# A decoder layer on one core: attention outputs turned by VectorE instead of TensorE, and maximum products placed between two score pairs

## Chip, cores and metric

The kernel runs on one NeuronCore of one Trainium2 chip. The metric is the device time of one launch in microseconds (us), the median of several runs. A batch of 8 sequences is worked on, all in float32 except where bfloat16 is named.

## The reference, cut to what matters

```python
x = _layernorm(x + _L0_attn_ref(x, ...))        # self-attention with decays by level
x = _layernorm(x + _L0_xattn_ref(x, ctx_1024, ctx_1024, Wq, Wk, Wv, Wo, bo))
x = _layernorm(x + _L0_ffn_ref(x, gate_w, gate_b, w1, w2))   # 32 experts, 8 tokens each

def _L0_xattn_ref(q, k, v, Wq, Wk, Wv, Wo, bo):  # 8 x 512 queries, 8 x 1024 keys, D = 256
    qh, kh, vh = ...                             # 16 heads of 16
    attn = softmax(einsum('bnhc,bmhc->bhnm', qh, kh) * 16 ** -0.5)
    return einsum('bhnm,bmhc->bnhc', attn, vh).reshape(B, QL, 256) @ Wo.T + bo
```

The gate of the last part takes a softmax over the 512 tokens of a batch for each of 32 experts and picks its 8 largest; each expert runs on its merged tokens, and the result is scattered back.

## The kernel before, in words

Three blocks follow each other: `self_attention`, `cross_attention`, `experts_and_combine`. In a block each engine has its own program, written out by hand, and they meet at semaphores; between blocks all engines meet. No planner sorts anything: the order of an engine's work is the order of the code.

The change sits almost wholly in `cross_attention`. Its `body` is called for the sections `pro`, `first` (batch 0), `mid` (batches 1 to 6), `last` (batch 7) and `tail` (what is left of batch 7). A batch is 32 steps `s`: four quads of heads (`q = s // 8`), eight chunks of 128 keys in each. In each step

- TensorE makes two score pairs (L1459: two heads each, transposed scores of 128 keys by 512 queries, into one of two slots `cpsA`), which ScalarE turns into probabilities (L1586, exp, 1.02 us a pair);
- TensorE makes four maximum products (L1398: queries by keys for step `s + 12`, `LEAD`), one at a time into one of three slots `cpsV`; VectorE takes the row maximum of each (L1680) and so empties the slot. Two of them stand behind the score pairs, two at the step's end;
- TensorE adds the values of the step before (L1420, four heads beside each other) into the one accumulator `acc`, 32 rows per head, 512 queries long. Every eighth step begins a new quad and needs `acc` empty.

The maxima of a quad go through a small chain (L1685 to L1701, then the transfer of `nmT` by SyncE, L1286) into three extra rows of the query stack, which the scores of that quad need 12 steps later; TensorE waits for that at steps 0, 8, 16 and 24.

When a quad is done, ScalarE copies `acc` to `OT` (L1616); one step later (`OUTPUTS = 1`) TensorE transposes it back to queries by features (L1439, four 128x128 blocks), VectorE divides by the row of sums (L1708, L1712) into `O`. At step 2 of the next batch (`MERGE`) TensorE transposes the whole `O` (L1360), ScalarE copies it to `oT` (L1558), and at step 4 (`PROJECT_O`) eight matmuls (L1475, four jobs, each needing a `cpsV` slot) give the output projection. VectorE adds the residual, the layer norm follows, then `X2T` (step 9: transposes of the normed tokens, L1522), `GATE` (step 12: two matmuls into 32 rows of 512, L1482; then the eight maxima, L1757), `TOP8` (step 20) and the picking of tokens (28, 29). The next batch is prepared beside it: `x1T` at step 0, the values of the second half of the heads at 1 (L1385), the queries at 4 (L1376), the keys at 7 and 12 (L1368), the values of the first half at 20. Each of these sends a 1024-wide result through a `cpsA` slot and a ScalarE copy of 1.01 us.

SyncE issues every transfer in one order, and waits in it: `stack_later` is twelve transfers that spread queries and keys of the next batch over the stack (L200, L201), `stack_max` is the transfer of `nmT`. In `last` and `tail` SyncE also loads the first experts' weights, 4 MB at a time (L1165).

## Time and profile before

| | |
|---|---|
| median of 3 runs (range) | 1839.48 us (1838.58 to 1839.82) |
| profiled execution: its time, its span | 1839.74 us, 1837.9 us |
| TensorE, VectorE, ScalarE, GpSimd busy | 91%, 67%, 46%, 33% of the span |
| mean granted TensorE clock | 0.953 of full speed |
| moved by transfers | 141.44 MB, mean 77 GB/s |

Self-attention lasts to about 589 us, the change of blocks to 629, the cross-attention's prologue to 660, batches 0 to 7 to 1643, the tail of batch 7 to 1677, the experts to 1804, the last layer norm to the end. A timeline row gives start, duration, engine, line, what is written and read, and in brackets how long the engine sat idle before it and whose end released it. `x4` merges four instructions; a busy TensorE overlaps its neighbours in these rows, so distances between starts are what to read.

### The profile page before, as it was taken

How to read it: one execution, taken by the hardware profiler on the slowest of the kernel's cores; microseconds unless marked ns; L12 is line 12 of the kernel's file. 1: busy time of each engine (PE TensorE's matmuls, PEld its weight loads, DVE VectorE, ACT ScalarE, POOL GpSimd, SP SyncE). 2: the span in 40 equal slices, each digit the busy share in tenths (PEclk: the TensorE clock that was granted, in tenths of full speed). 3: DMA queues.
4: the chain of work that ended last, by engine and by line, in shares of the span. 5: the costliest groups of instructions: out<-in, count | busy, mean ns of one | idle time of the engine just before them, and what ended most of it. 6: DMA issues, size and time to landing. Idle time of an engine off the chain costs nothing. (4 is left out here: it accounts for less than half of the span.)

```text
span 1837.9 us, 48963 instructions
## 1 busy us (share of the span) xinstructions
PE 1678.5 (91%) x19924; PEld 806.8 (44%) x19924; DVE 1232.9 (67%) x2424; ACT 838.3 (46%) x1015; POOL 598.2 (33%) x970
## 2 busy tenths in 40 slices
PE   5999999999999699999999999999999999976564
PEld 3566666666665333343333433433433334223332
DVE  5767677677674777868778788788687787812005
ACT  2334344344333136655646565566556465651103
POOL 3545545645625536043043061250430420000002
PEclk8999999999999779999999999999999999987777
DMA  7000000000000221111202101112112024046995
GB/s 252 3 4 4 3 3 3 3 3 3 3 32 15 69 67 50 41 38 59 83 1 85 56 28 65 50 38 69 35 64 78 1 89 183 30 179 267 421 418 183
DMA packets 62205, 141.44 MB, mean 77 GB/s; under 512 B 11280, under 2 KB 34320, under 8 KB 54320
## 3 DMA queue, kind: packets, MB, share of 16 engines
q1 hardware_dynamic: 61520, 137.88, 20.6%
q8 instruction: 157, 2.57, 0.6%
q10 hardware_dynamic: 480, 0.59, 0.1%
q14 instruction: 48, 0.39, 0.1%
HBM read 92.43 MB, written 7.86 MB: 55 GB/s over the span
## 5 line engine op out<-in xcount | busy, mean ns | idle before, releaser
L1680 DVE TENSOR_REDUCE mx<-cpsV 128x1 f32<-128x512 f32 x1024 | 655.2, 686 | 187.5 <-PE cpsV L1398 175.3
L1586 ACT ACTIVATE w<-cpsA 128x1024 f32<-128x1024 f32 x512 | 496.3, 1021 | 246.0 <-PE cpsA L1459 240.8
L1398 PE MATMUL cpsV<-w 96*128 96x512 bf16 x1024 | 325.4, 394 | 21.6 <-DVEq L1663 13.0
L1459 PE MATMUL cpsA<-w 99*128 99x512 bf16 x1024 | 275.2, 382 | 22.4 <-DMA w<-nmT 10.1
L1420 PE MATMUL cacc<-w 128*32 128x512 f32 x2048 | 279.7, 607 | 0.4 <-ACT w L1586 0.4
L468 PE MATMUL psA<-w 128*128 128x512 f32 x512 | 257.0, 625 | 5.0 <-DVE WT L1102 1.8
L1398 PEld LDWEIGHTS cpsV<-w 96*128 96x128 bf16 x1024 | 86.1, 98 | 283.4 <-DVE mx L1680 197.0
L1648 POOL TENSOR_TENSOR crstd<-cmv,eps 128x4 f32<-128x4 f32 x8 | 1.6, 202 | 605.8 <-DVE cmv L1746 605.8
L765 ACT COPY w<-psA 128x1024 f32<-128x1024 f32 x64 | 64.8, 1012 | 229.3 <-PE psA L468 229.3
L1459 PEld LDWEIGHTS cpsA<-w 99*128 99x128 bf16 x1024 | 93.0, 98 | 163.0 <-ACT w L1564 15.8
L885 POOL TENSOR_TENSOR VP<-V,VPF 128x128 f32<-128x128 f32 (+2 forms) x256 | 129.2, 535 | 42.7 <-PE psA L481 36.8
L1111 DVE TENSOR_TENSOR tmp<-psV,CF 128x512 f32<-128x512 f32 x64 | 44.3, 692 | 121.7 <-PE psV L531 121.4
L468 PEld LDWEIGHTS psA<-w 128*128 128x128 f32 x512 | 87.9, 191 | 76.5 <-issue 67.7
L183 POOL TENSOR_TENSOR w<-w,zero 128x256 bf16<-128x256 f32 x88 | 51.1, 612 | 138.8 <-ACTq L1565 138.8
L1420 PEld LDWEIGHTS cacc<-w 128*32 128x32 f32 x2048 | 42.5, 108 | 92.5 <-issue 74.5
L2031 DVE TENSOR_TENSOR z<-psE,b1T 128x256 f32<-128x256 f32 x8 | 3.4, 424 | 110.5 <-PE psE L1967 110.5
L1981 PE MATMUL psE<-w,hT 128*32 128x256 f32 x512 | 39.6, 477 | 36.5 <-DMA w<-in_w 34.6
L1564 ACT COPY w<-cpsA 128x1024 f32<-128x1024 f32 x21 | 21.3, 1012 | 111.5 <-PE cpsA L1368 59.9
L1118 DVE TENSOR_REDUCE w<-tmp 128x128 f32<-128x512 f32 x64 | 67.8, 1059 | 4.7
L501 PEld LDWEIGHTS psV<-w 64*32 64x32 f32 x4096 | 41.2, 106 | 49.8 <-issue 48.1
L1385 PEld LDWEIGHTS cpsA<-w,w 128*128 128x128 f32 x480 | 54.7, 192 | 12.6 <-ACT w L1586 12.6
L192 POOL TENSOR_TENSOR w<-w 128x256 bf16<-128x256 f32 x88 | 57.1, 680 | 3.1
(224 smaller groups left out, 2227.6 us busy)
## 6 DMA issues: line engine op xcount, KB each, us to landing
w<-in_w SPq DMA_DIRECT2D x56, 1024.0 KB, 16.3
w<-w SPq DMA_DIRECT2D x189, 128.0 KB, 2.3
w<-w SPq DMA_DIRECT2D x189, 64.0 KB, 2.0
w<-in_ctxT SPq DMA_DIRECT2D x8, 1024.0 KB, 5.0
w<-in_xT SPq DMA_DIRECT2D x8, 512.0 KB, 6.4
x_tok<-in_x SPq DMA_DIRECT2D x8, 512.0 KB, 9.7
w<-in_w SPq DMA_DIRECT2D x8, 512.0 KB, 17.2
out_y<-w SPq DMA_DIRECT2D x16, 256.0 KB, 2.3
```

What stands on the lines that cost most here:

```text
L183: ops.tensor_tensor(cut(high, m), cut(r, m), zeros, ALU.add)
L192: ops.tensor_tensor(cut(low, m), cut(r, m), cut(mid, m), ALU.subtract)
L468: last = nc.tensor.matmul(out[:, n * T:(n + 1) * T], w[:, k, i * P:(i + 1) * P], XT[:, b, k, :], start=(k == 0), stop=(k == KD - 1))
L765: nc.scalar.copy(QK[:, i % 4, :], full(("qk", i))).then_inc(act_evac, 1)
L885: last = nc.gpsimd.tensor_tensor(VP[:, p % 2, g, 0:n, :].rearrange("q n (h c) -> q n h c", c=HD), vv.unsqueeze(1).broadcast_to([P, n, 2, HD]),
L1118: nc.vector.tensor_reduce(yp, tmp[:].rearrange("p g s c -> p g c s"), AX_X, ALU.add)
L1385: last = nc.tensor.matmul(out[:, c * P:(c + 1) * P], cT[:, k, c * P:(c + 1) * P], wv[:, k, hv * P:(hv + 1) * P], start=(k == 0), stop=(k = ...
L1398: nc.tensor.matmul(out, Qst[q // 2][0:ROWS, hh, g * P:(g + 1) * P], Kst[q // 2][0:ROWS, hh, half * BANK:(half + 1) * BANK], start=True, st ...
L1420: last = nc.tensor.matmul(acc[BLK * jj:BLK * (jj + 1), :], Vc[:, chunk, 4 * q + jj, :], Pr[:, (2 * s + jj // 2) % 4, (jj % 2) * T:(jj % 2 ...
L1459: last = nc.tensor.matmul(out[:, n * T:(n + 1) * T], Kst[q // 2][0:ROWS + 3, hh, chunk * P:(chunk + 1) * P], Qst[q // 2][0:ROWS + 3, hh, : ...
L1586: nc.scalar.activation(Pr[:, (2 * s + pp) % 4, :], src, ACT.Exp, scale=CA_SCALE).then_inc(act_evac, 1)
L1680: nc.vector.tensor_reduce(mx[:, q % 2, row, k % 2:k % 2 + 1], full(m[k]), AX_X, ALU.max).then_inc(dve_evac, 1)
```

## The change

The outputs of a quad are no longer transposed by TensorE. The values of a head are laid at every second column of its 32 (with the ones at column 1). After the quad's last step VectorE reads `acc` itself and transposes it in 32x32 blocks to `byq` (`take_outputs`); this also frees `acc`. Later (`outputs`) it divides and transposes back to `byd`, and SyncE moves 64 of the 128 rows to their place in `oT` (`move_o`). The divisions of quads 0 to 3 stand at steps 12 and 20 of the batch, and both at step 1 of the next (in `last`, quad 2 at step 27). The output projection is two jobs instead of four. The gate's product is four groups of 32 rows by 128, at step 11, brought to 32 rows of 512 by four transfers before the maxima at step 12. The transposes of `X2T` are two jobs. In steps 1, 2, 5, 8, 10, 13 and 21 the first two maximum products stand between the two score pairs. The store of `x2` to memory moves ahead of the third `nmT` transfer. In the tail TensorE runs 130 transposes whose results nobody reads. In the tail of self-attention GpSimd adds `lnb` ahead of its norm factors, and VectorE multiplies by `lng` instead of GpSimd.

```diff
-OUTPUTS, X1T, PROJECT_V1, PROJECT_Q, MERGE, PROJECT_O, NORM = 1, 0, 1, 4, 2, 4, 7
-PROJECT_K, X2T, COPY_X2, GATE, GATE_EXP, TOP8, TOP8_T, PICK, PICK_T = (7, 12), 9, 10, 12, 14, 20, 21, 28, 29
-PROJECT_V0 = 20
+X1T, PROJECT_V1, PROJECT_Q, PROJECT_O, NORM = 0, 1, 4, 4, 7
+PROJECT_K, X2T, COPY_X2, GATE, GATE_MAX, GATE_EXP, TOP8, TOP8_T, PICK, PICK_T = (7, 12), 9, 10, 11, 12, 14, 20, 21, 28, 29
+PROJECT_V0, LAST_OUTPUTS = 20, 27
+BEHIND_JOBS = (X1T + 1, PROJECT_V1 + 1, PROJECT_Q + 1, PROJECT_K[0] + 1, X2T + 1, PROJECT_K[1] + 1, PROJECT_V0 + 1)
...
+                    if sec == "tail" and r == 0:
+                        pool.wait_ge(dve_evac, SA_DVE.count(sec, b, ("out", 1)) + DVE_SLOTS)
+                        add_lnb()
...
-                        dve.wait_ge(n1_scaled, b)
+                        if sec == "tail":
+                            dve.wait_ge(n1_ready, b * 2 - 1)
+                            nc.vector.tensor_tensor(n1[:], n1[:], lng[:].unsqueeze(1).broadcast_to([P, G, D]), ALU.mult)
+                            dve.drain()
+                        else:
+                            dve.wait_ge(n1_scaled, b)
...
-        if s % KT == OUTPUTS and (now and s > KT or prev and s < KT):
-            v.append(("otr", (s // KT - 1) % QUADS))
         if prev:
-            v += [("wo", g) for g in range(G) if s == PROJECT_O]
+            v += [("wo", r) for r in range(2) if s == PROJECT_O]
...
+        byq = [sb(f"byq_{n}", [P, KT * 2, BLK]) for n in range(2)]
+        byd = [sb(f"byd_{n}", [P, T]) for n in range(2)]
+        rec = sb("rec", [P, KT * 2])
...
+            def move_o(bb, q):
+
+                sp.wait_ge(o_ready, bb * QUADS + q + 1)
+                sp.dma_start(oT[64 * (q % 2):64 * (q % 2) + 64, q // 2, :], byd[q % 2][0:P:2]
+                             ).then_inc(o_moved[q % 2], 16)
...
+                if prev:
+                    if sec != "tail":
+                        move_o(b - 1, 2)
+                    move_o(b - 1, 3)
+                if now:
...
+                    sp.wait_ge(l4_ready, b)
+                    for g in range(G):
+                        sp.dma_start(L[:, g * P:(g + 1) * P], L4[E * g:E * (g + 1)]).then_inc(l_moved, 16)
...
                     stack_max(b, 2)
+                    move_o(b, 0)
...
                     sp.dma_start(sh.p8_dram[:, bass.ds((b - 1) * T, T)], P8).then_inc(p8_saved, 16)
                 if now:
+                    move_o(b, 1)
                     if nxt:
                         stack_later(b + 1, 1, free=CA_ACT.count(sec, b, ("s", 16, 1)))
...
                         stack_max(b + 1, 0)
                     else:
+                        move_o(b, 2)
                         sp.wait_ge(act_full, CA_ACT.count(sec, b, ("s", STEPS - 1, 1)))
                         load_group_weights(sp, sh, dram, 1, 1, EG)
                         sp.wait_ge(av_done, B * STEPS)
...
+                def keep_clock(count):
+
+                    if sec == "tail":
+                        for _ in range(count):
+                            nc.tensor.transpose(acc[:, 0:P], sh.ident[:], sh.ident[:])
...
+                            if maxima and pp == (0 if s in BEHIND_JOBS else 1):
+                                max_scores(s + LEAD, 0, 1)
+
+                    if sec == "tail" and s == 1:
+                        pe.wait_ge(acc_evac, b * QUADS + 1)
+                        keep_clock(34)
...
-                            evacuated_a("oT")
-                            for g in range(G):
-                                out = take_v(("wo", g))
-                                for k in range(KD):
-                                    last = nc.tensor.matmul(out[:, 0:D], oT[:, k, g * P:(g + 1) * P], wo[:, k, :],
-                                                            start=(k == 0), stop=(k == KD - 1))
+                            for of in o_moved:
+                                pe.wait_ge(of, b * 32 + 16)
+                            for r in range(2):
+                                out = take_v(("wo", r))
+                                for g in range(2):
+                                    for k in range(KD):
+                                        last = nc.tensor.matmul(out[:, g * D:(g + 1) * D],
+                                                                oT[:, k, (2 * r + g) * P:(2 * r + g + 1) * P], wo[:, k, :],
+                                                                start=(k == 0), stop=(k == KD - 1))
                                 last.then_inc(dve_full, 1)
+                            keep_clock(28)
...
+                            evacuated_a(("x2T", 1))
                             for k in range(KD):
-                                last = nc.tensor.matmul(out[0:E, :], gw[:, k, :], x2T[:, k, :],
-                                                        start=(k == 0), stop=(k == KD - 1))
+                                for g in range(G):
+                                    last = nc.tensor.matmul(out[E * g:E * (g + 1), 0:P], gw[:, k, :],
+                                                            x2T[:, k, g * P:(g + 1) * P], start=(k == 0), stop=(k == KD - 1))
                             last.then_inc(dve_full, 1)
+                            keep_clock(52)
...
-                    if prev and s == MERGE:
-                        pe.wait_ge(o_ready, b * QUADS)
-                        transpose_x("oT", O)
...
-                        nc.scalar.copy(OT[:], acc[:]).then_inc(acc_evac, 1)
...
+                def take_outputs(bb, q):
+
+                    dve.wait_ge(av_done, (bb * QUADS + q + 1) * KT)
+                    nc.vector.transpose(byq[q % 2][:].rearrange("p c s -> p (c s)"), acc[:]).then_inc(acc_evac, 1)
                     dve.drain()
-                    ov = O[:].rearrange("p g (h c) -> p g h c", c=HD)
-                    for g in range(G):
-                        last = nc.vector.tensor_tensor(ov[:, g, 4 * q:4 * q + 4], src[:, g, :, 0:HD],
-                                                       rec[:, g].unsqueeze(2).broadcast_to([P, 4, HD]), ALU.mult)
-                    dve.drain().then_inc(o_ready, 1)
-                    dve.nop().then_inc(dve_evac, 1)
+
+                def outputs(bb, q):
+
+                    t = byq[q % 2]
+                    nc.vector.reciprocal(rec[:], t[:, :, 1])
+                    dve.drain()
+                    nc.vector.tensor_tensor(t[:, :, 0:BLK:2], t[:, :, 0:BLK:2], rec[:].unsqueeze(2).broadcast_to([P, KT * 2, HD]),
+                                            ALU.mult)
+                    dve.drain()
+                    dve.wait_ge(o_moved[q % 2], bb * 32 + (q // 2 + 1) * 16)
+                    nc.vector.transpose(byd[q % 2][:], t[:].rearrange("p c s -> p (c s)")).then_inc(o_ready, 1)
...
+                    if prev and s == 1:
+                        if sec != "tail":
+                            outputs(b - 1, 2)
+                        outputs(b - 1, 3)
...
+                            nc.vector.tensor_scalar(L4[:], full("lg")[:, 0:P], gb[:, 0:1], None, ALU.add
                                                     ).then_inc(dve_evac, 1)
-                            dve.drain()
+                            dve.drain().then_inc(l4_ready, 1)
+                        if s == GATE_MAX:
+                            dve.wait_ge(l_moved, b * (16 * G))
+                            if now:
+                                outputs(b, 0)
...
+                    if sec == "first" and s == GATE_MAX:
+                        outputs(b, 0)
+                    if now and s == TOP8:
+                        outputs(b, 1)
+                    if sec == "last" and s == LAST_OUTPUTS:
+                        outputs(b, 2)
...
+                    if now and s and s % KT == 0:
+                        take_outputs(b, s // KT - 1)
+                    if prev and s == 0:
+                        take_outputs(b - 1, 3)```

On **TensorE**, steps 1 to 3 of a middle batch; L1360 with `O` is the merge, L1439 the transposes of a quad, L1385 the values' projection. Before:

```order
L1459 MATMUL cpsA<-w_0 128x512 x4
L1398 MATMUL cpsV<-w_0 128x512 x2
L1439 MATMUL cpsV<-ident,OT 128x128 x4
L1420 MATMUL cacc<-w_1 32x512 x4
L1385 MATMUL cpsA<-w_1,w_0 128x128 x16
L1398 MATMUL cpsV<-w_0 128x512 x2
L1459 MATMUL cpsA<-w_0 128x512 x4
L1398 MATMUL cpsV<-w_0 128x512 x2
L1420 MATMUL cacc<-w_1 32x512 x4
L1360 MATMUL cpsA<-ident,O 128x128 x8
L1398 MATMUL cpsV<-w_0 128x512 x2
```

With the change (L1491 are the scores, L1430 the maximum products, L1452 the values, L1417 the projection):

```order
L1491 MATMUL cpsA<-w_0 128x512 x2
L1430 MATMUL cpsV<-w_0 128x512 x2
L1491 MATMUL cpsA<-w_0 128x512 x2
L1452 MATMUL cacc<-w_1 32x512 x4
L1417 MATMUL cpsA<-w_1,w_0 128x128 x16
L1430 MATMUL cpsV<-w_0 128x512 x2
L1491 MATMUL cpsA<-w_0 128x512 x2
L1430 MATMUL cpsV<-w_0 128x512 x2
L1491 MATMUL cpsA<-w_0 128x512 x2
L1452 MATMUL cacc<-w_1 32x512 x4
L1430 MATMUL cpsV<-w_0 128x512 x2
```

Both kinds of transposes are gone, and two maximum products stand between the halves of the scores.

On **SyncE**, from step 20 of a middle batch, with the semaphores it waits on; `p_scratch` is the store of the gate's result, the `16x4` rows are the twelve transfers of `stack_later`. Before:

```order
L1319 DMA p_scratch<-P 32x512
L200 DMA w_0<-w_0 16x4x1024 [waits ca_act_full]
L201 DMA w_0<-w_0 16x4x512
...
L1286 DMA w_1<-nmT 3x16x128 [waits ca_nmt_ready]
```

With the change:

```order
L1349 DMA p_scratch<-P 32x512
L1303 DMA oT<-byd 64x512 [waits ca_o_ready]
L201 DMA w_0<-w_0 16x4x1024 [waits ca_act_full]
L202 DMA w_0<-w_0 16x4x512
...
L1297 DMA w_1<-nmT 3x16x128 [waits ca_nmt_ready]
```

The twelve transfers and `nmT` now stand behind a wait for quad 1's outputs.

On **SyncE**, the end of `last` and the tail. Before:

```order
L1319 DMA p_scratch<-P 32x512 [waits ca_p8]
L1165 DMA w_0<-in_w 128x2048 [waits ca_act_full]
L1165 DMA w_0<-in_w 128x2048 x3
L1286 DMA w_1<-nmT 3x16x128 [waits ca_nmt_ready]
L1165 DMA w_1<-in_w 128x2048 [waits ca_act_full]
L1165 DMA w_1<-in_w 128x2048 x3
L1165 DMA w_1<-in_w 128x2048 [waits ca_av_done]
```

With the change:

```order
L1303 DMA oT<-byd 64x512 [waits ca_o_ready]
L1174 DMA w_0<-in_w 128x2048 [waits ca_act_full]
L1174 DMA w_0<-in_w 128x2048 x3
L1297 DMA w_1<-nmT 3x16x128 [waits ca_nmt_ready]
L1303 DMA oT<-byd 64x512 [waits ca_o_ready]
L1174 DMA w_1<-in_w 128x2048 [waits ca_act_full]
L1174 DMA w_1<-in_w 128x2048 x3
L1174 DMA w_1<-in_w 128x2048 [waits ca_av_done]
L1174 DMA w_1<-in_w 128x2048 x3
L1303 DMA oT<-byd 64x512 [waits ca_o_ready]
L1333 DMA L<-L 32x128 [waits ca_l4]
```

The move of the last quad stands behind both weight loads; before, nothing of the tail's chain went over SyncE.

## Rows read from the trace of the kernel before

**Rows 1.** Stretches: length, busy PE, PEld, DVE, ACT, POOL, clock, DMA share, GB/s.

```profile
778.00:904.00 126.00, 122.91 (x686) 48.05 (x683) 97.82 (x198) 72.86 (x79) 35.74 (x58) 1.00 0.16 53
1677.00:1804.00 127.00, 87.49 (x976) 44.56 (x975) 4.04 (x10) 15.69 (x25) 2.54 (x9) 0.83 0.98 397
```

**Rows 2.** Timeline of TensorE and VectorE around a quad's end, steps 16 and 17.

```profile
847.81 0.60 PE L1398 MATMUL cpsV<-w 96*128 96x512 bf16 x2
850.64 0.61 PE L1398 MATMUL cpsV<-w 96*128 96x512 bf16 x2
854.00 0.61 PE L1398 MATMUL cpsV<-w 96*128 96x512 bf16 x2
...
851.07 2.59 DVE L1680 TENSOR_REDUCE mx<-cpsV 128x1 f32<-128x512 f32 x4 [0.25 <-PE cpsV L1398]
```

**Rows 3.** Groups by line, VectorE's transposes in self-attention: count, busy us, mean ns.

```profile
L1047 DVE STREAM_TRANSPOSE w<-w 128x1024 f32<-128x1024 f32 x16 | 19.9, 1245 | 1.2
L991 DVE STREAM_TRANSPOSE w<-w 128x2048 f32<-128x2048 f32 x8 | 18.5, 2311 | 0.6
```

**Rows 4.** Timeline of TensorE, steps 2 and 3 of batch 2.

```profile
915.84 1.09 PE L1360 MATMUL cpsA<-ident,O 128*128 128x128 f32 x8
917.21 0.60 PE L1459 MATMUL cpsA<-w 99*128 99x512 bf16 x2
918.04 0.60 PE L1459 MATMUL cpsA<-w 99*128 99x512 bf16 x2 [0.24 <-ACT oT L1558]
```

**Rows 5.** Timeline of TensorE, the output projection of batch 6.

```profile
1550.73 1.10 PE L1475 MATMUL cpsV<-cwo,oT 128*128 128x256 f32 x4
...
1555.13 1.07 PE L1420 MATMUL cacc<-w 128*32 128x512 f32 x8
```

**Rows 6.** Timeline of VectorE, step 12 of batch 1.

```profile
839.25 1.29 DVE L1680 TENSOR_REDUCE mx<-cpsV 128x1 f32<-128x512 f32 x2 [2.13 <-PE cpsV L1398]
```

**Rows 7.** Timeline of SyncE and TensorE, steps 20 to 24 of batch 1.

```profile
865.63 0.57 SPq L200 DMA_DIRECT2D w<-w  x1
...
874.08 0.77 SPq L1286 DMA_DIRECT2D w<-nmT  x1
...
876.33 1.04 PE L1459 MATMUL cpsA<-w 99*128 99x512 bf16 x4 [0.18 <-DMA w<-nmT]
```

**Rows 8.** Timeline of TensorE, step 13 of the last batch.

```profile
1586.37 0.39 PE L1398 MATMUL cpsV<-w 96*128 96x512 bf16 x1 [1.09 <-DVE mx L1680]
1587.29 1.88 PE L1420 MATMUL cacc<-w 128*32 128x512 f32 x8
```

**Rows 9.** Timeline of VectorE and ScalarE at the end of self-attention.

```profile
604.50 1.23 DVE L192 TENSOR_TENSOR w<-w 128x1024 bf16<-128x1024 f32 x1
616.09 3.21 DVE L192 TENSOR_TENSOR w<-w 128x1024 bf16<-128x1024 f32 x1
626.36 2.07 ACT L725 ACTIVATE x_tok<-w,shift,rstd 128x256 f32<-128x256 f32 x4
```

**Rows 10.** Timeline of SyncE and TensorE, step 24 of the last batch.

```profile
1612.23 3.35 SPq L1165 DMA_DIRECT2D w<-in_w  x4
1615.62 0.73 SPq L1286 DMA_DIRECT2D w<-nmT  x1
...
1625.11 1.89 PE L1459 MATMUL cpsA<-w 99*128 99x512 bf16 x4 [7.45 <-DMA w<-nmT]
```

**Rows 11.** The tail: one stretch, then the timeline of SyncE and TensorE.

```profile
1643.00:1665.00 22.00, 13.69 (x55) 8.30 (x55) 5.85 (x21) 5.03 (x6) 1.21 (x2) 0.71 0.93 381
1643.21 4.27 SPq L1165 DMA_DIRECT2D w<-in_w  x8
1650.49 6.26 PE L1475 MATMUL cpsV<-cwo,oT 128*128 128x256 f32 x16 [1.10 <-ACT oT L1558]
1663.67 3.59 PE L1482 MATMUL cpsV<-x2T,gw 128*32 128x512 f32 x4 [1.19 <-ACT x2T L1558]
1676.90 3.65 PE L1950 MATMUL psE<-w,mg 128*32 128x512 f32 x20 [1.43 <-POOL mg L1894]
```

More of the change, by code:

```diff
@@ L951, in body @@
                         level_logits()
[L952 removed]
+                    if i == 4 and prev and sec != "tail":
                         add_lnb()
@@ L1191, in ca_jobs @@
         if prev:
-            a += {MERGE: ["oT"], X2T: ["x2T"]}.get(s, [])
+            a += [("x2T", k) for k in range(KD) if s == X2T]
         if nxt:
@@ L1450, in body @@
                     q, chunk = s // KT, s % KT
+                    maxima = now and (nxt or s + LEAD < STEPS)
                     if now:
```

98 lines of the change are left out of this document (43 added, 55 removed).

## The prediction

> **What bounds the kernel now.** I read first the stretches, to see which engine is full where; then the timeline of one middle batch step by step, since the batches repeat; then SyncE's own timeline, since the change puts new waits there; last the chain through the tail.
>
> In a middle batch of 126 us TensorE is busy for 122.9, VectorE for 97.8, at a granted clock of 1.00 [rows 1]. VectorE's share misleads: in a step without a projection the same two products come back after 2.83 us, and VectorE's four maxima take 2.59 of them and leave 0.25 idle, waiting for TensorE [rows 2]. So TensorE bounds these steps, but VectorE can take in only about 0.25 us more a step; time for it is found where TensorE does a projection and needs no maxima, as the 2.13 us of idling in step 12 show [rows 6]. SyncE is a third bound at one place: at step 24 TensorE waits for the transfer of `nmT`, which is queued behind twelve others [rows 7]. The experts keep the transfer engines busy for a share of 0.98 at 397 GB/s [rows 1]: they end a fixed time after they begin, and whatever delays the tail delays the end.
>
> **The change part by part**, per middle batch (there are six), minus being faster.
>
> Merge: its transposes hold TensorE for 0.93 us (915.84 to the next row), and the ScalarE copy behind them opens a gap between the score pairs: 0.83 us from pair to pair where 0.44 is undisturbed, so 0.39 [rows 4]. Both go: **-1.3**. ScalarE's copies go too, at no price, since it is busy for 73 of 126 us [rows 1].
>
> Output projection: 4.40 us until the values follow [rows 5]; the same sixteen records took 6.26 at half clock in the tail [rows 11], so 3.1 to 3.4 without waits for slots. Two jobs find their slots free: **-1.0**.
>
> Products between the pairs: the gap of 0.39 exists behind each projection, and two products of 0.44 together fill it. Of seven places, one (step 1) has no gap in most batches, one (13) is counted with the gate, one (21) is swallowed by the wait at step 24. Four stay: **-1.5**.
>
> Quad's end: the four transposes made one step 3.36 us long instead of 2.83 [rows 2]: 0.53 goes. In their place VectorE empties the accumulator. Its transposes cost 1.04 ns per element of a row and 0.18 us (2311 less 1245 over 1024) [rows 3]; 512 make 0.71 us. It can begin when the maxima of the step are done, 851.07 + 1.30 = 852.37, and ends at 853.1; TensorE wants the accumulator at about 852.4 (850.64, then 0.44 of products, 0.87 of scores, 0.44 of products). A wait of 0.75 to 0.8 for 0.53 saved, +0.2, four times: **+0.8**. The Trainium skill says against this part ("VectorE: DVE Perf Modes", Rules for kernel authors) that a 128x128 transpose belongs to TensorE where its result may lie in PSUM; by that rule both passes of VectorE would be paid in full, and that is the third rival.
>
> The rest of an output (reciprocal, product over 256, second transpose: 0.25 + 0.4 + 0.71, with the drains 1.55 us) lies in steps 1, 12 and 20 beside projections of some 3.5 us. At step 1 twice 1.55 just fits, at 20 it fits. At 12 it doesn't quite. The gate's product, 3.59 us at half clock [rows 11], is 1.8 at full clock; as four groups side by side I estimate 0.5, as eight value records in four groups take 1.07 [rows 5]. That shortens TensorE's step 11 and 12 by 1.3, and so VectorE's window too: 2.13 idle [rows 6], plus 0.4 for an add of 128 instead of 512 columns, less 1.55, less 1.3, is -0.3, and the four transfers can cost up to 0.5 more. With the products of step 13 now ahead of its second score pair, this lateness delays both: of 1.3 + 0.4 I keep **-0.5** (bounds -1.6 and +0.6).
>
> SyncE: at step 20 the twelve transfers and `nmT` come behind the move of quad 1, and that behind VectorE's 1.55 us. With 0.6 to issue the move and 0.5 less for the gate's store, which now runs beside the wait, they are 1.6 later. From 865.63 to 874.08 they take 8.45, and TensorE goes on 2.25 after the last [rows 7]. Three batches already wait there, three have some 0.4 us to spare, which the gain of step 21 eats: **+1.5**. Below nothing it can't be, for nothing makes `nmT` earlier.
>
> Clock: such a wait lasts about 2 us. Behind one of 1.09 us the values took 1.88 [rows 8] instead of 1.07 [rows 5], the lower of the two clock levels; with the products and scores of that step I put it at 1.7 (0.8 is the row's own). Another wait of similar length left the clock up. Half of the times: **+0.8** (0 to 1.7).
>
> Sum -1.2 a batch, **-7.2** for six. Batch 0 has no merge and no projection: 1.9 of gaps saved, 0.6 + 0.8 + 0.5 lost: **0**.
>
> Last batch: 8 MB of weights are issued at its start ahead of quad 1's `nmT`, so step 8 is fixed by them and the gains of steps 2 to 7 become a longer wait (clock +0.9). Step 12 has no projection to hide VectorE's extra work: +1.8. The next 4 MB and `nmT` behind them [rows 10] leave 1.6 later. Small terms -0.4. Together **+3.9**.
>
> Self-attention's end: VectorE's passes there took 3.21 instead of 1.23 [rows 9], while GpSimd worked on `lnb` and `lng`. With that moved, the two slow ones end 4.2 us earlier, ScalarE's transfers follow, and its last norm, now at 626.36 [rows 9], ends some 4 us earlier: **-3.9** (-2.5 to -4.5). The prologue behind it only shifts.
>
> **Tail.** The move of the last quad stands behind eight weight transfers issued from 1643.21, 8.4 MB at 381 GB/s, drained at about 1665 [rows 11]. What that means the trace shows once: `nmT`, issued at 1615.62 behind 4 MB issued from 1612.23, released TensorE at 1625.11, 9.5 us later [rows 10], against 2.25 without such a load [rows 7]. So the projection begins at 1665.2 instead of 1650.49 [rows 11]: +14.7. Behind it: gate product -2.8, transposes in two halves and a higher clock from the idle transposes -2.4, add -0.4, wider residual adds +0.3, four transfers of the gate 3 x 0.4 + 2.25 = +3.4; -1.9. Together **+12.8**. The 34 idle transposes end long before 1665, so the projection starts at the lower level, as now. The experts' first row, 1676.90 [rows 11], moves with it, and the end too.
>
> Sum: -3.9 + 0 - 7.2 + 3.9 + 12.8 = +5.6. The profiled execution took 1839.74, 0.26 above the median of the runs: **1845.0**.
>
> **Rivals.** A: the small transfer overtakes the weights. The Trainium skill ("DMA: Bandwidth & Descriptors", Queues, rings and completion order) says that completion is not first in, first out for an issuing engine; by it this could happen. Here two of the last batch's `nmT` transfers waited for the load's end, one of them in [rows 10], so I give it little. The 14.7 go: 1830.3.
>
> B: steps 12 and 24 cost nothing, if VectorE keeps up and the wait for `nmT` falls together with others and never lowers the clock: -3.5 a batch, 1831.2. For it: three batches have slack at step 24. Against: the order of SyncE fixes the wait.
>
> C: VectorE becomes the bound: both its passes show, 1.42 for 0.53 at 24 quads, 21 us less the 4.8 counted: 1861. Against it are the windows beside projections; it decides if VectorE's idle 0.25 a step is gone everywhere.
>
> **Chances.** Forecast 0.70, A 0.12, B 0.12, C 0.06. 0.2% is 3.7 us, about what a measurement of this kernel can tell from no change; the border to slower is 1843.2. The forecast's own bounds (gate -1.6 to +0.6 and clock 0 to 1.7 in six batches, 1.4 at the transition) give 1837 to 1853, and about three quarters of it lie above the border, a little under 1835.8. Slower 0.57, the same 0.17, faster 0.26. The range 1830 to 1853 takes in A and B and leaves C and the forecast's upper end out.
>
> **What would show it.** In the tail, TensorE's row of the output projection at about 1665 minus the shift of what is ahead, released by the transfer of `byd`, with the load's stretch at a share near 1 before it; if it begins 5 us after the last values, A is right. At step 24 of each middle batch a wait of about 2 us for `nmT`, SyncE's twelve transfers ending in front of it. At a quad's end 0.8 us of TensorE waiting for VectorE's transpose of `cacc`. Middle batches of about 124.5 instead of 125.6 us. The cross-attention's first product near 625 instead of 629. It would be wrong if the batches became longer, or the tail shorter than now.

## The result, and the profile after

The changed kernel takes **1850.99 us** (median of 4 runs, 1849.02 to 1853.02) against 1839.65 (4 runs, 1838.58 to 1840.27): ratio 1.0062, 95% interval 1.0045 to 1.0080. It is slower, 6 us beyond the forecast of 1845.0 and within its range. The profiled execution's span is 1850.4 us, against 1837.9.

Where the 12.5 us between the spans lie. The marks are the first values' projection of batch 0 (before 667.79, now 664.15), of batch 1 (782.69, 779.69) and of batch 7 (1537.80, 1530.24), the last values (1644.53, 1640.42), the experts' first product (1676.90, 1687.36) and the end.

| stretch | before | now | difference | forecast |
|---|---|---|---|---|
| to the first projection of batch 0 | 667.79 | 664.15 | -3.6 | -3.9 |
| batch 0 | 114.90 | 115.54 | +0.6 | 0 |
| batches 1 to 6 | 755.11 | 750.55 | -4.6 | -7.2 |
| batch 7 | 106.73 | 110.18 | +3.5 | +3.9 |
| tail | 32.37 | 46.94 | +14.6 | +12.8 |
| experts and last norm | 161.00 | 163.04 | +2.0 | 0 |

The stretches of the changed kernel that answer to [rows 1] and [rows 11] (length, busy PE, PEld, DVE, ACT, POOL, clock, DMA share, GB/s):

```profile
780.00:905.00 125.00, 119.17 (x660) 45.02 (x658) 101.21 (x192) 69.45 (x74) 35.75 (x58) 0.99 0.17 56
1640.00:1662.00 22.00, 5.05 (x46) 3.85 (x42) 2.11 (x4) 0.36 (x1) 0.00 (x0) 0.70 0.94 387
1687.00:1815.00 128.00, 85.09 (x963) 43.02 (x963) 3.82 (x9) 15.70 (x25) 3.00 (x10) 0.81 0.97 394
```

TensorE lost almost 4 us of work in a batch (119.2 instead of 122.9) and VectorE gained 3.4, yet the batch is only 0.8 shorter. The second row is the tail's hole: the transfer engines full, TensorE busy for 5 of 22 us.

The tail's chain over all engines, against [rows 11]:

```profile
1640.42 1.06 PE L1452 MATMUL cacc<-w 128*32 128x512 f32 x8 [0.36 <-ACT w L1623]
1642.32 3.93 PE L1471 MATMUL cacc<-ident 128*128 128x128 f32 x34 [0.84 <-DVE byq L1742]
1643.93 0.48 SPq L1303 DMA_DIRECT2D oT<-byd  x1
1662.38 5.38 PE L1509 MATMUL cpsV<-cwo,oT 128*128 128x256 f32 x16 [16.13 <-issue]
1675.40 2.50 SPq L1333 DMA_DIRECT2D L<-L  x4
1679.14 0.68 DVE L1802 MAX8 m<-L 32x8 f32<-32x512 f32 x1 [3.81 <-DMA L<-L]
```

The move of the last quad is issued at 1643.93 and the projection that needs it begins at 1662.38. Its wait is put down to "issue", so the row doesn't name the releaser; the runs below do. The 34 idle transposes are over by 1646.3, 16 us too early to help.

Waits inside the batches, TensorE of batch 1 and of batch 7, against [rows 2, 7, 10]:

```profile
817.56 1.06 PE L1452 MATMUL cacc<-w 128*32 128x512 f32 x8 [0.58 <-DVE byq L1742]
872.48 1.04 PE L1491 MATMUL cpsA<-w 99*128 99x512 bf16 x4 [1.63 <-DMA w<-nmT]
873.88 1.93 PE L1452 MATMUL cacc<-w 128*32 128x512 f32 x8
1558.00 0.60 PE L1491 MATMUL cpsA<-w 99*128 99x512 bf16 x2 [1.50 <-DMA w<-nmT]
1620.94 1.89 PE L1491 MATMUL cpsA<-w 99*128 99x512 bf16 x4 [9.43 <-DMA w<-nmT]
```

The first is a quad's end, 0.58 us of waiting for VectorE's transpose. The second is step 24; behind it the values took 1.93 us instead of 1.06, the lower clock level. In the other middle batches that wait is 0.62, 0.62, 1.58, 1.10 and 0.64 us, and only behind the 1.58 one the clock fell again.

### The profile page after: what moved, and what is told of

Its sections match the earlier page's. It is cut to its first block and busy times, and to the rows that moved or that the text cites. A ratio compares the mean times of both kernels' runs of the same rounds, so it can differ in the third digit from the quotient of the medians.

```text
span 1850.4 us, 49002 instructions
## 1 busy us (share of the span) xinstructions
PE 1660.7 (90%) x19958; PEld 799.5 (43%) x19958; DVE 1261.3 (68%) x2377; ACT 819.2 (44%) x983; POOL 594.6 (32%) x969
## 3 DMA queue, kind: packets, MB, share of 16 engines
q8 instruction: 158, 2.59, 0.6%
## 5 line engine op out<-in xcount | busy, mean ns | idle before, releaser
L1714 DVE TENSOR_REDUCE mx<-cpsV 128x1 f32<-128x512 f32 x1024 | 655.1, 686 | 151.7 <-PE cpsV L1430 125.5
L1623 ACT ACTIVATE w<-cpsA 128x1024 f32<-128x1024 f32 x512 | 499.5, 1021 | 288.6 <-PE cpsA L1491 283.1
L1430 PE MATMUL cpsV<-w 96*128 96x512 bf16 x1024 | 333.6, 396 | 34.1 <-DVE mx L1714 24.0
L1491 PE MATMUL cpsA<-w 99*128 99x512 bf16 x1024 | 276.2, 382 | 17.4 <-DMA w<-nmT 17.1
L1452 PE MATMUL cacc<-w 128*32 128x512 f32 x2048 | 275.9, 611 | 15.8 <-DVE byq L1742 8.1
L1430 PEld LDWEIGHTS cpsV<-w 96*128 96x128 bf16 x1024 | 85.5, 98 | 320.5 <-DVE mx L1714 237.1
L1491 PEld LDWEIGHTS cpsA<-w 99*128 99x128 bf16 x1024 | 96.4, 98 | 139.6 <-DMA w<-nmT 22.0
L1452 PEld LDWEIGHTS cacc<-w 128*32 128x32 f32 x2048 | 42.6, 108 | 117.4 <-issue 83.6
L1417 PEld LDWEIGHTS cpsA<-w,w 128*128 128x128 f32 x480 | 54.7, 192 | 12.6 <-ACT w L1623 12.6
```

What stands on the lines that cost most here:

```text
L1417: last = nc.tensor.matmul(out[:, c * P:(c + 1) * P], cT[:, k, c * P:(c + 1) * P], wv[:, k, hv * P:(hv + 1) * P], start=(k == 0), stop=(k = ...
L1430: nc.tensor.matmul(out, Qst[q // 2][0:ROWS, hh, g * P:(g + 1) * P], Kst[q // 2][0:ROWS, hh, half * BANK:(half + 1) * BANK], start=True, st ...
L1452: last = nc.tensor.matmul(acc[BLK * jj:BLK * (jj + 1), :], Vc[:, chunk, 4 * q + jj, :], Pr[:, (2 * s + jj // 2) % 4, (jj % 2) * T:(jj % 2 ...
L1491: last = nc.tensor.matmul(out[:, n * T:(n + 1) * T], Kst[q // 2][0:ROWS + 3, hh, chunk * P:(chunk + 1) * P], Qst[q // 2][0:ROWS + 3, hh, : ...
L1623: nc.scalar.activation(Pr[:, (2 * s + pp) % 4, :], src, ACT.Exp, scale=CA_SCALE).then_inc(act_evac, 1)
L1714: nc.vector.tensor_reduce(mx[:, q % 2, row, k % 2:k % 2 + 1], full(m[k]), AX_X, ALU.max).then_inc(dve_evac, 1)
```

## The experiments

Medians of the kernel before moved between 1836.9 and 1839.65 us from one set of runs to the next, and in the kernels with the changed self-attention the first projection of batch 0 came anywhere from 659.3 to 664.9 us, though nothing ahead of it differs. Whole times therefore tell apart some 3 us. The steps tell more: from one step's values row of TensorE to the next the distance repeats within 0.02 us in most places. Two places are rougher. Steps 13 and 14 together took 11.01 to 11.51 us, and steps 24 and 25 took 7.62 to 8.12, in six kernels whose middle batches have the same code (the changed one, move_act, both_act, load_behind, tail_gate, tg_no_clock). This table has those distances, the mean over batches 1 to 6. "24, 25" are steps 24 and 25 together.

| step (what stands there) | before | changed | behind_none | nmt_first | all_in | take_act |
|---|---|---|---|---|---|---|
| 2 (values' projection) | 6.91 | 6.59 | 6.96 | 6.59 | 6.59 | 7.77 |
| 3 (merge) | 4.16 | 2.84 | 2.83 | 2.83 | 2.83 | 2.83 |
| 4 (output projection) | 7.30 | 6.80 | 6.80 | 6.80 | 6.80 | 6.77 |
| 5 (queries' projection) | 6.85 | 7.05 | 6.85 | 7.05 | 6.85 | 6.85 |
| 8 (keys' projection) | 6.84 | 6.45 | 6.84 | 6.45 | 6.46 | 6.46 |
| 9, 17 (quads' ends) | 6.72 | 6.92 | 6.92 | 6.92 | 6.92 | 5.67 |
| 10 (X2T) | 4.16 | 3.85 | 3.79 | 3.85 | 3.79 | 3.79 |
| 11 to 14 (gate, keys) | 17.03 | 17.11 | 16.89 | 17.12 | 16.64 | 17.33 |
| 21 (values' projection) | 7.35 | 7.62 | 7.40 | 7.62 | 7.40 | 8.06 |
| 24, 25 (nmT, quad's end) | 6.60 | 7.95 | 8.12 | 6.42 | 6.32 | 5.67 |
| whole batch | 125.85 | 125.09 | 125.29 | 123.55 | 122.46 | 122.31 |

The steps left out are the same everywhere within 0.05 us (the pair at a batch's change in take_act apart).

And the tail: from the last values to the output projection, from there to the experts' first product, and from there to the end.

| | to projection | to experts | to the end |
|---|---|---|---|
| before | 5.96 | 26.41 | 161.0 |
| changed | 21.96 | 24.98 | 163.0 |
| move_act | 11.35 | 25.23 | 163.1 |
| both_act | 11.55 | 27.81 | 163.3 |
| load_behind | 6.18 | 33.17 | 163.2 |
| tail_gate | 6.18 | 23.47 | 161.0 |
| tg_no_clock | 6.35 | 26.71 | 161.0 |

### The last quad's transfer on another queue

```diff
+ # scalar engine, tail, step 1; taken out of SyncE's list
+ act.wait_ge(o_ready, b * QUADS)
+ act.dma_start(oT[64:128, 1, :], byd[1][0:P:2]).then_inc(o_moved[1], 16)
```

> The transfer of the last quad's outputs is issued by ScalarE, which is idle then, instead of by SyncE behind eight weight transfers; all else as in the changed kernel. Theory Q (the transfer waits because it is queued behind the weights on SyncE): the output projection begins about 4 us after the transpose into byd, near 1648 instead of 1662.4, and the whole shortens by 13 to 15 us, to about 1837. Theory S (the 16 transfer engines are full at that time, whoever issues): it begins near 1662 as before and the time stays 1851. Between: it shares the engines with the weights packet by packet and lands 2 to 6 us after its issue, 1838 to 1842.

1842.38 us (10 runs, 1839.01 to 1848.27) against 1837.27 (23 runs): ratio 1.0028 (1.0015 to 1.0042). ScalarE's queue and TensorE, then the stretch:

```profile
1646.74 0.54 ACTq L1619 DMA_DIRECT2D oT<-byd  x1
1654.57 5.61 PE L1509 MATMUL cpsV<-cwo,oT 128*128 128x256 f32 x16 [5.51 <-issue]
1644.00:1656.00 12.00, 5.65 (x42) 4.88 (x39) 2.11 (x4) 0.00 (x0) 0.00 (x0) 0.82 1.01 401
```

The projection follows the issue by 7.8 us, neither the 18.5 of the changed kernel nor the 2.6 of an empty queue: the small transfer now passes the weights but shares 16 full engines with them. So Q is right for 11 us and sharing takes 5; the sharing came out a little dearer than the "between" case. The whole is 8.6 us below the changed kernel by the medians, 6.2 when each is set against its own runs of before.

### The gate's transfers there too

```diff
+ # scalar engine, tail, step 11; taken out of SyncE's list
+ for g in range(G):
+     act.dma_start(L[:, g * P:(g + 1) * P], L4[E * g:E * (g + 1)]).then_inc(l_moved, 16)
```

> As the run with the last quad's transfer on ScalarE, and the four transfers of the gate's product in the tail are issued by ScalarE too. Theory Q: if they came early enough to find the weights still in SyncE's queue, this takes off up to 2 us more than the first run (about 1836); issued after the weights have drained (some 22 us after 1640, so 1662) both are alike. Theory S: 1851, like the first run.

1843.70 us (10 runs, 1838.86 to 1849.95), ratio 1.0033 (1.0017 to 1.0048): not told apart from the run before, as Q says for transfers issued at 1666, when the weights are gone. The maxima start 4.29 us after VectorE's add ended, against 3.82 in move_act: nothing is won, and ScalarE needs 2.97 us to issue the four where SyncE needs 2.50. The maxima's delay of 0.47 us even grew on its way. TensorE's wait for `P` behind it was 2.02 us instead of 1.56, the granted clock fell after it (0.68 in the stretch 1670:1680, where move_act has 1.00), and the way to the experts took 27.81 us instead of 25.23. The tail of nmt_first below, the same code as the changed kernel's, shows this too: 4.32 us, then 27.85.

### The weights behind the last quad's transfer

```diff
  move_o(b - 1, 3)                     # SyncE, tail
+ load_group_weights(sp, sh, dram, 1, 1, EG)     # both were ahead of it, in the last batch
+ load_group_weights(sp, sh, dram, 2, 1, EG)
```

> Both 4 MB weight loads at the end of the last batch are issued behind the last quad's transfer on SyncE; all transfers stay on SyncE. Theory Q: the projection begins near 1648, the loads run from about 1644.5 to 1666, the gate's four transfers, issued near 1660, land behind them at about 1668 instead of 1678, and the whole takes about 1841. Theory A of the prediction (a small transfer overtakes the weights of the same queue): the gate's transfers land about 2.5 us after their issue and it takes about 1836. If the weights then come too late for the first experts: a wait for w in the first group and over 1843.

1844.56 us (8 runs, 1836.89 to 1848.21), ratio 1.0030 (1.0011 to 1.0048). SyncE, TensorE and VectorE of the tail:

```profile
1644.30 0.47 SPq L1303 DMA_DIRECT2D oT<-byd  x1
1646.90 3.69 PE L1510 MATMUL cpsV<-cwo,oT 128*128 128x256 f32 x16 [0.35 <-issue]
1658.24 2.50 SPq L1336 DMA_DIRECT2D L<-L  x4
1669.46 0.68 DVE L1803 MAX8 m<-L 32x8 f32<-32x512 f32 x1 [11.29 <-DMA L<-L]
```

The projection starts 2.6 us after the issue, and now at full clock: 3.69 us for its sixteen matmuls where the changed kernel took 5.38. What was won there, the next small transfers pay: issued at 1658.24 behind 8 MB, they let the maxima start 11.2 us later. This is the cleanest sight of the queue: the same engine, once with and once without weights ahead. Rival A of the prediction falls with it.

### Nothing of the tail's chain behind the weights

```diff
  # as load_behind, and for the tail
+ if sec == "tail":
+     nc.tensor.matmul(out[0:E, :], gw[:, k, :], x2T[:, k, :], start=(k == 0), stop=(k == KD - 1))
...
+ nc.vector.tensor_scalar(L[:], full("lg")[0:E, :], gb[0:E, 0:1], None, ALU.add)   # no L4, no transfers
```

> As the run with both weight loads behind the last quad's transfer, and in the tail the gate's product is made as before the change (two matmuls of 512 into 32 rows), so that it needs no transfers. Theory Q: with nothing of the tail's chain behind the weights, the eight maxima start near 1661 instead of 1669.5, and the whole takes 8 to 9 us less than load_behind, about 1836. Rival (the experts' small transfers or the weights, drained only at 1666, hold the first group): 2 to 4 us less, about 1841.

1831.70 us (10 runs, 1827.84 to 1843.95), ratio 0.9976 (0.9958 to 0.9994), 5.6 us faster than before. VectorE and TensorE:

```profile
1649.51 3.69 PE L1510 MATMUL cpsV<-cwo,oT 128*128 128x256 f32 x16 [0.34 <-issue]
1659.71 1.88 PE L1520 MATMUL cpsV<-x2T,gw 128*32 128x512 f32 x4 [0.16 <-ACT x2T L1635]
1662.46 0.68 DVE L1812 MAX8 m<-L 32x8 f32<-32x512 f32 x1
1672.98 4.98 PE L2015 MATMUL psE<-w,mg 128*32 128x512 f32 x32 [1.80 <-POOL mg L1959]
```

The tail is 29.65 us from the last values to the experts, 17.3 shorter than in the changed kernel and 2.7 shorter than before. The wide gate product costs 1.88 us at full clock, the narrow one 0.64 and then 3.8 of transfers.

### The idle transposes

```diff
- if sec == "tail":
+ if False:
      for _ in range(count):
          nc.tensor.transpose(acc[:, 0:P], sh.ident[:], sh.ident[:])
```

> As tail_gate, without the 130 transposes of the tail whose results nobody reads. Theory K (they hold TensorE's clock at its upper level through a chain that now has no long wait in it): projection 3.7 to about 6 us, transposes of the normed tokens 1.6 to 1.9, gate's product up by 1 to 2: 4 to 6 us slower than tail_gate, about 1841. Rival (the waits between the products drop the clock whatever runs between): within 1 us of tail_gate.

1835.59 us (10 runs, 1831.13 to 1839.33), ratio 0.9991 (0.9980 to 1.0002), 3.9 more than tail_gate by the medians. Its profiled span is shorter (1829.4), because the first projection of its batch 0 came at 659.3; from the last values on it is 3.4 us longer:

```profile
1641.72 6.46 PE L1510 MATMUL cpsV<-cwo,oT 128*128 128x256 f32 x16 [5.29 <-DMA oT<-byd]
1655.20 3.59 PE L1520 MATMUL cpsV<-x2T,gw 128*32 128x512 f32 x4 [0.77 <-ACT x2T L1635]
1635.00:1668.00 33.00, 16.59 (x53) 8.93 (x52) 11.18 (x29) 3.24 (x6) 1.53 (x3) 0.64 0.64 260
```

The stretch that answers to it in tail_gate:

```profile
1643.00:1673.00 30.00, 24.60 (x185) 19.71 (x186) 11.18 (x29) 3.10 (x6) 1.92 (x5) 0.99 0.70 287
```

The granted clock is 0.64 without the idle transposes and 0.99 with them. Theory K holds for the clock, a little under its price of 4 to 6 us. With the transposes gone TensorE's wait has a name in the trace too: the transfer of `byd`.

### Where the maximum products stand

```diff
- BEHIND_JOBS = (X1T + 1, PROJECT_V1 + 1, PROJECT_Q + 1, PROJECT_K[0] + 1, X2T + 1, PROJECT_K[1] + 1, PROJECT_V0 + 1)
+ BEHIND_JOBS = ()
```

> The maximum products stand behind the two score pairs in all steps, as before the change; all else as in the changed kernel. Theory R (the reordering gains 0.3 to 0.4 us at steps 2, 8 and 10 and loses 0.2 to 0.4 at steps 5, 13 and 21, where VectorE is late and the products between the pairs delay the second pair): steps 2, 8 and 10 get longer by 0.3 to 0.4 each, steps 5, 13 and 21 shorter by 0.2 to 0.4, and the whole stays within 1.5 us of 1851. The prediction's own count (0.39 at four places, nothing lost elsewhere): 9 us longer, 1860. Rival (steps 5, 13 and 21 are longer because VectorE's outputs hold up the slots whatever the order): those three keep their length, and the whole is 6 to 7 us longer, 1857.

1852.36 us (4 runs, 1849.62 to 1852.68); by its own runs of before 1.0072 (1.0055 to 1.0089), by the spans 0.5 us more than the changed kernel. Not the 9 us of the prediction's count. By the table, steps 2 and 8 win 0.37 and 0.39 through the new order, step 10 loses 0.06, steps 5, 13 with 14, and 21 lose 0.20, 0.22 and 0.22, and steps 24 and 25 win 0.17: together the new order wins 0.2 us a batch. Two of these are rough. In batch 3 VectorE waits at step 12 for the gate's four transfers, 0.80 us in the changed kernel and 0.54 here, and steps 13 and 14 take 11.75 and 12.68 us; in the other five batches they take 10.86 and 10.42, so that the order costs 0.44 there. And 0.17 is less than steps 24 and 25 scatter between kernels with the same code. So the new order is worth 0.2 us a batch at most. Theory R is right but for step 10: its gap of 0.37 is gone with the products behind as well, and the two halves of `X2T` are what else changed there. Why step 5 loses, in the changed kernel (TensorE, then VectorE):

```profile
799.87 0.22 PE L1439 MATMUL cpsV<-identb,NM 128*128 128x128 bf16 x1
800.61 0.39 PE L1430 MATMUL cpsV<-w 96*128 96x512 bf16 x1
801.20 0.39 PE L1430 MATMUL cpsV<-w 96*128 96x512 bf16 x1 [0.21 <-DVE mx L1714]
801.43 0.60 PE L1491 MATMUL cpsA<-w 99*128 99x512 bf16 x2
799.86 1.29 DVE L1714 TENSOR_REDUCE mx<-cpsV 128x1 f32<-128x512 f32 x2 [2.75 <-PE cpsV L1430]
```

At steps 5, 13 and 21 the transpose of a quad's maxima (L1439) stands behind the projection and takes a `cpsV` slot as well; at steps 2, 8 and 10 none does. With the two products ahead of it, all three slots are taken at 799.87. The next two products must each wait until VectorE has emptied one, and the second score pair stands behind them and goes at 801.43. VectorE isn't late here: it had idled for 2.75 us when the first product came. With the products behind, the same pair goes 0.85 us after the first instead of 1.50. That the third slot decides is read from these rows; no run moved the transpose.

### SyncE's order at step 24

```diff
- move_o(b, 1)
  stack_later(b + 1, 1, ...)
  stack_max(b, 3)
+ move_o(b, 1)
```

> The transfer of quad 1's outputs is issued behind the twelve transfers of the stack and nmT of quad 3, instead of in front of them; all else as in the changed kernel. Theory N (that transfer's wait for VectorE is what makes nmT late at step 24): steps 24 and 25 of a middle batch together fall from 7.95 to about 6.6 us, the drops of the clock behind the wait go, -1.3 in six batches and -1.6 in the last, together 8 to 10 us: about 1842. Rival (the chain to nmT starts at the same time anyway, since it follows the gate's store at step 20): steps 24 and 25 stay at 7.9 and the whole at 1851.

1844.30 us (8 runs, 1842.62 to 1846.27), ratio 1.0036 (1.0022 to 1.0050); its span, 1842.0, is 8.4 below the changed kernel's. By the medians it is 6.7 below, 4.3 when each is set against its own runs of before; the way from the projection to the experts, 2.9 us longer at the lower clock, hides part of what the batches won. Steps 24 and 25 take 6.42 us. SyncE in batch 1, first the changed kernel (store of the gate's result, the move, nmT), then this one:

```profile
859.60 0.36 SPq L1349 DMA_DIRECT2D p_scratch<-P  x1
860.85 0.52 SPq L1303 DMA_DIRECT2D oT<-byd  x1
870.19 0.76 SPq L1297 DMA_DIRECT2D w<-nmT  x1
```

```profile
860.04 0.36 SPq L1349 DMA_DIRECT2D p_scratch<-P  x1
869.38 0.76 SPq L1297 DMA_DIRECT2D w<-nmT  x1
870.18 0.54 SPq L1303 DMA_DIRECT2D oT<-byd  x1
```

From the store to `nmT` it is 10.59 and 9.34 us: the wait for VectorE and the issue of the move cost 1.25 us of SyncE. Theory N holds.

### The self-attention's end alone

The four pieces of the diff in self-attention's tail, put into the kernel before.

> The kernel before with nothing but the change to self-attention's tail (GpSimd adds lnb ahead of its norm factors, VectorE multiplies by lng). Expected: the distance from the end of self-attention's last product to the cross-attention's first one shrinks and the whole is 3.6 us faster than before (-2.5 to -4.5). Rival (the start of the cross-attention is set by the stack's transfers or the cut of keys, and the 3.6 us seen in the changed kernel are the spread of self-attention from run to run): within 1 us of before.

1834.55 us (10 runs, 1829.87 to 1838.05), ratio 0.9986 (0.9974 to 0.9998): 2.4 us by the medians, with an interval that reaches from nothing to 4.8. The trace is sharper. Before, `L192` took 3.21 us beside GpSimd's work [rows 9], and TensorE's first product waited 12.97; here:

```profile
613.44 1.23 DVE L189 TENSOR_TENSOR w<-w,zero 128x1024 bf16<-128x1024 f32 x1
614.75 1.23 DVE L192 TENSOR_TENSOR w<-w 128x1024 bf16<-128x1024 f32 x1
625.57 6.83 PE L1406 MATMUL cpsV<-w 96*128 96x512 bf16 x12 [8.84 <-DVEq L1671]
```

4.1 us less, in two passes that run at 1.23 again.

### A version that beats both

```diff
  # as tail_gate, and on SyncE
+ stack_max(b, 3)                      # ahead of the twelve transfers, or of 4 MB of weights
  stack_later(b + 1, 1, ...)
+ move_o(b, 1)
...
+ stack_max(b, 1)                      # last batch: ahead of 8 MB
  load_group_weights(sp, sh, dram, 1, 0, 0)
...
+ if sec == "last" and s == TOP8:      # instead of step 12
+     outputs(b, 0)
...
+ BEHIND_JOBS = (PROJECT_V1 + 1, PROJECT_K[0] + 1)
```

> As tail_gate; nmT of quad 3 goes ahead of the twelve transfers of the stack (in the middle batches) and of the 4 MB of weights (in the last one), nmT of quad 1 goes ahead of the 8 MB of the last batch, the last batch's outputs of quad 0 move from step 12 to step 20, and the products stand between the score pairs only at steps 2 and 8. Expected against tail_gate (1836): step 24 and 25 of a middle batch 6.3 instead of 7.95, steps 5, 13 and 21 shorter by 0.7 together, so -2.2 in six batches (13); last batch: step 24 at 2.9 instead of 12.3, step 8 at 2.9 instead of 4.5, step 13 and 14 about 4 us shorter (14). Sum -27: about 1810. If VectorE or the later weight loads take the place of these waits: 1820 to 1830.

**1803.50 us** (4 runs, 1803.25 to 1804.72), ratio 0.9815 (0.9794 to 0.9837): 33.8 us faster than its own runs of before, where the changed kernel was 11.3 slower than its. Middle batches take 122.46 us instead of 125.09, step 24 of the last batch 2.70 instead of 12.32 and its step 8 3.88 instead of 4.50. One piece failed: with quad 0's output moved to step 20, steps 13 to 15 of the last batch were to lose 4 us and take 14.95 instead of 15.44. The four transfers of the gate still hold VectorE at step 12 (0.53 us of waiting); gate_wide below shows what that costs. The parts of this version were not run one by one.

### The same order in the kernel before

```diff
+ stack_max(b, 3)
  stack_later(b + 1, 1, ...)           # or 4 MB of weights
...
+ stack_max(b, 1)                      # last batch
  load_group_weights(sp, sh, dram, 1, 0, 0)
```

> The kernel before, with SyncE's order of all_in: nmT of quad 3 ahead of the twelve transfers of the stack (middle batches) and ahead of 4 MB of weights (last batch), nmT of quad 1 ahead of 8 MB of the last batch. It tells how much of all_in's gain the kernel before could have had too. Expected: step 24 of the middle batches 2.83 instead of 3.24 on average (-2.4 in six), step 24 of the last batch 2.8 instead of 10.3 and step 8 shorter by 0.8 (-8): about 1828 against 1838. Rival (all_in's gain is in this order alone): below 1815.

1827.82 us (4 runs, 1823.86 to 1830.25), ratio 0.9944 (0.9923 to 0.9964): 9.1 of all_in's 33.8 us were there to be had without the change. Its middle batches take 125.40 us. So with `nmT` in time on both sides, outputs by VectorE, the narrow gate and the two placed products are worth 2.94 us a batch.

### The accumulator emptied by ScalarE

```diff
+ nc.scalar.copy(OT[q % 2][:], acc[:]).then_inc(acc_evac, 1)      # ScalarE, at the quad's end
...
+ nc.vector.transpose(t[:].rearrange("p c s -> p (c s)"), OT[q % 2][:])   # VectorE, in outputs
```

> As all_in, but the accumulator is emptied by ScalarE's plain copy into a buffer, as before the change, and VectorE makes its first 32x32 transpose from that buffer later, with the rest of the output. Theory V (at a quad's end TensorE waits for VectorE, which can begin only after the step's maxima): steps 9, 17 and 25 fall from 3.48 to 2.83 us, 0.65 at each of four quads' ends; VectorE's 0.7 us come back at steps 2, 13 and 21 where its window is full, up to 0.7 each and twice that at step 2. Net -0.5 to -2.6 a batch, 4 to 18 us in all: 1786 to 1800. Rival (the 0.65 us are the accumulator's turn-round whoever empties it): steps 9, 17, 25 stay at 3.48, the later steps grow, 1804 to 1815.

1802.17 us (4 runs, 1798.88 to 1803.67) against all_in's 1803.50: not told apart. The table says why: steps 9, 17 and 25 fall by 0.65, 0.60 and 0.65 us and step 1, the fourth quad's end, by 0.69; step 2 grows by 1.18, 11 to 14 by 0.69 and 21 by 0.66. TensorE in step 2:

```profile
781.01 0.38 PE L1433 MATMUL cpsV<-w 96*128 96x512 bf16 x1
782.39 0.39 PE L1433 MATMUL cpsV<-w 96*128 96x512 bf16 x1 [1.00 <-DVE mx L1728]
```

Theory V is right about the wait and wrong in hope: a microsecond of VectorE's work has to be paid somewhere.

### The gate's product wide again

The diff of tail_gate's gate, for every batch.

> As all_in, but the gate's product is made in every batch as before the change (two matmuls of 512 into 32 rows, at step 11), with no transfers behind it. It separates the gate's part of the change from the rest. Prediction's count: TensorE's work at full clock 1.9 instead of 0.5 us, but VectorE's window at steps 11 to 13 grows as much and its add is 0.4 longer: steps 11 to 14 together, 16.6 us in all_in, become 17.0 to 17.5, 2 to 6 us slower in seven batches, 1806 to 1810. Rival (VectorE's window is what is short there, so that TensorE's extra work is hidden, and the four transfers cost TensorE a wait now): 16.6 or less, 1801 to 1804.

1806.53 us (4 runs, 1805.53 to 1811.02), ratio 0.9841 (0.9823 to 0.9858). Steps 11 to 14 take 17.77 us instead of 16.64, above the 17.0 to 17.5 expected: step 11 is 0.43 and step 12 0.83 longer, while step 13, where VectorE is behind, gives back only 0.13. TensorE's extra work isn't hidden there, and the narrow product is worth 1.1 us in a middle batch (1.3 in five of them, 0.5 in batch 3 with its wait for the four transfers).

In the last batch the narrow product costs time. Steps 11 to 15 take 21.06 us in all_in and 18.43 here. TensorE at steps 13 and 14, first all_in, then this one:

```profile
1559.94 0.39 PE L1432 MATMUL cpsV<-w 96*128 96x512 bf16 x1 [1.68 <-DVE mx L1720]
1565.30 1.94 PE L1454 MATMUL cacc<-w 128*32 128x512 f32 x8
```

```profile
1566.16 0.39 PE L1428 MATMUL cpsV<-w 96*128 96x512 bf16 x1 [1.06 <-DVE mx L1711]
1569.91 1.07 PE L1450 MATMUL cacc<-w 128*32 128x512 f32 x8
```

Without the transfers VectorE's maxima start without a wait, TensorE's wait for a slot is 0.6 us shorter, and the values behind it take 1.07 us instead of 1.94: the clock stays at the upper level (1.00 in 1567:1574, where all_in has 0.57 in 1561:1568). Steps 13 to 15 take 11.07 us instead of 14.95: the 4 us that all_in was to win there, and still 2.6 net of the wider product's 1.3 at steps 11 and 12.

## Why the prediction was right, and where its terms were not

**Tail, +12.8; measured +14.6.** Right in mechanism and place; the term of 14.7 for the move was mis-sized and is 16.0. It counted 22.0 us from the first of the eight weight issues to the projection (1643.21 to 1665.2 in [rows 11]). In the changed kernel SyncE begins them 4.1 us earlier, as TensorE arrives 4.1 us earlier, and the projection follows after 23.3 us (1639.09 to 1662.38). The rest, counted as -1.9, is -1.4; in nmt_first, where the clock fell once more, the same code gives +1.4. Load_behind shows that it is the queue; by the Trainium skill's page "DMA: Bandwidth & Descriptors" (Queues, rings and completion order), from which rival A came, a transfer may complete ahead of an earlier one of the same engine. No run here shows one that did.

**Products between the pairs, -1.5 at steps 2, 5, 8 and 10; measured -0.5.** This is the step that failed. The prediction took the gap of 0.39 behind every projection as won. At steps 2 and 8 it was. At 5, 13 and 21 the transpose of the maxima holds the third slot, and there the order ties the second score pair to a slot that VectorE must empty first. The prediction saw the tie at step 13, where VectorE is late besides, and didn't ask for it at 5 and 21, where the slots alone make it. At step 10 the two halves of `X2T` had removed the gap already, a gain of 0.37 that wasn't in the sum. Over the whole batch the new order is worth 0.2 us at most.

**Merge -1.3**: -1.32. **Output projection -1.0**: -0.50. From the start of the sixteen matmuls to the next row it is 3.92 us in batch 1, where 3.1 to 3.4 were counted. A part of this is the count: in load_behind's tail, where no maxima want a slot, it is 3.53 at full clock (1646.90 to 1650.43). The remaining 0.4 fits the small chain of VectorE's maxima, which comes first (790.92 to 792.30 in batch 1).

**Gate -0.5**: steps 11 to 14 are 0.1 longer on average, in three parts. In five of the six batches they take 16.52 us with the products behind, against 17.03 before: the gate with its output is worth 0.5, as forecast. The order takes back 0.44 of it. In batch 3 the wait for the four transfers makes the steps 0.8 longer than before. In gate_wide, with the product as wide as before, they are 0.75 longer than before, which fits VectorE's output of quad 0 at step 12; that output was not tried alone in a middle batch.

**Quad's end, +0.2 each**: +0.12 at steps 9 and 25, +0.08 at 17, with a wait of 0.58 us instead of 0.75 to 0.8; about +0.3 a batch instead of +0.8. The page "VectorE: DVE Perf Modes" of the Trainium skill (Rules for kernel authors) would have had the transposes stay on TensorE; here the row of 0.58 us replaced 0.53 us of TensorE's own work, and the output path as a whole belongs to the 2.94 us a batch that all_in wins over before_order. Rival C, in which both passes show in full, is out: a quad's end grew by 0.1 us.

**SyncE +1.5 and clock +0.8**: steps 24 and 25 together are +1.35, and nmt_first takes 1.53 off. The wait was forecast as some 2 us and is 0.6 to 1.6; the clock fell in two of six batches, not in half of them. With step 21 (+0.27, forecast as swallowed) and without the quad's end they are +1.5 for a forecast of 2.3.

So the middle batch's -1.2 was -0.76: order, output projection and gate were taken 2.1 us too well, the quad's ends and the wait at step 24 1.3 us too badly, and 0.37 came unforeseen.

**Last batch +3.9**: +3.5. Steps 11 to 14 lose 2.4 (forecast 1.8), step 24 2.0 (1.6), step 8 waits 1.50 us. **Self-attention's end -3.9**: -3.8 at the first product (628.89 to 625.10), and turn_only confirms the two passes as its place.

**Experts, counted as nothing: +2.0.** That stays open. In the changed kernel TensorE waits once for the experts' small transfers, and SyncE issues its first weight load 6.5 us after the experts' first product instead of 5.6:

```profile
1694.38 1.97 PE L2022 MATMUL psE<-ident,hS 128*128 128x128 f32 x8 [2.38 <-DMA b<-in_w]
```

By the tail's table the four transfers of the gate could be the cause. But before_order, which has none in its tail, takes 162.8 us from the experts' first product to the end, and nmt_first, which has them, 161.7. The 2 us come in two parts of about 1 us, one ahead of the first load and one behind it, each there in some kernels and not in others, and no run ties either to an edit.

## What to carry to other kernels

Ask of every small transfer that a change adds what its queue already holds at that moment: one 128 KB move behind 8 MB of weights cost three times what six batches had gained, and it cost nothing once the weights stood behind it. Before moving a job ahead, count every job that takes one of the shared slots: the same two products gained 0.4 us at two places and lost 0.2 to 0.4 at three, where one more job held a slot. On an engine that is second in line, count free time by place, not by sum: VectorE idles a fifth of a batch, and 0.7 us moved to it from one place still came back at the next. When whole times scatter by a few microseconds, measure distances between rows that repeat.

## What the runs showed that was not expected

A small transfer on another engine's queue, against 8 MB under way on the first, took 7.8 us from its issue to the product that needs it, 2.6 without such a load and 18.5 behind it on the same queue: a second queue passes the waiting bytes, not the busy engines. The idle transposes are there to keep the clock up in the tail. The first 34 do not reach that where the wait behind them is 16 us: the changed kernel's projection takes 5.38 us, in load_behind, with 0.35 us of waiting, 3.69. All 130 together bring 3.4 us where the chain has no long wait (tail_gate against tg_no_clock).
